# Spreading routing weights over channels by products with a constant 0/1 matrix, in the last stage of a cross-attention and expert kernel

## What is computed

```python
xn = layernorm(x)                                  # x: 8 x 224 x 512
d2 = sum(xn*xn) + sum(p*p) - 2 * xn @ prototypes.T # 32 prototypes
w  = softmax(-sqrt(max(d2, 0)) / t)
topw, topi = top_k(w, 2); topw /= sum(topw)
for slot in range(2):
    h = B[topi[slot]] @ xn                         # rank 16
    y = A[topi[slot]] @ h + bias[topi[slot]]
    out += topw[slot] * y
return x + out
```

## Time and profile before

| what | value |
|---|---|
| median of 3 runs | 996.6 us (992.65 to 997.54) |
| profiled execution: its own time | 998.39 us |
| its span, first to last instruction | 996.7 us |
| mean granted clock of TensorE | 0.967 |
| busy in the span: PE, DVE, ACT, POOL | 90%, 63%, 49%, 25% |
| last stage | from about 798 us to the end |

### The profile page before, as it was taken

One profiled execution on the slowest core, in us unless ns is written; L12 is line 12 of the kernel. 1 busy time (PEld: TensorE's weight loads), 2 busy tenths in 40 slices (PEclk: granted clock), 3 DMA queues, 4 the chain that ended last, 5 costly groups with the idle time before them and its releaser, 6 DMA issues. The chain is left out here.

```text
span 996.7 us, 18525 instructions
## 1 busy us (share of the span) xinstructions
PE 896.3 (90%) x6480; PEld 768.8 (77%) x6480; DVE 628.5 (63%) x1466; ACT 486.6 (49%) x1055; POOL 248.4 (25%) x208
## 2 busy tenths in 40 slices
PE   4899999999999759998899998999999858999996
PEld 4798998989989647777777777777777648788884
DVE  3743643735537068888678887888888645666662
ACT  4211301212212057778677786777787624443431
POOL 0740340621415000033103040033332222223400
PEclk9899999999999969999899998999999978999999
DMA  9646546366444656667756667666778321111201
GB/s 263 213 164 228 193 153 233 135 205 219 173 145 168 167 165 137 145 155 160 155 123 148 149 144 154 147 150 141 184 173 200 91 77 37 57 55 58 70 19 37
DMA packets 96288, 144.36 MB, mean 145 GB/s; under 512 B 7605, under 2 KB 57429, under 8 KB 96226
## 3 DMA queue, kind: packets, MB, share of 16 engines
q1 hardware_dynamic: 93362, 133.56, 49.3%
q0 software_dynamic: 2864, 10.00, 3.7%
HBM read 91.98 MB, written 51.54 MB: 144 GB/s over the span
## 5 line engine op out<-in xcount | busy, mean ns | idle before, releaser
L879 PE MATMUL prob_ps<-ident,scores 112*125 112x112 f32 x1536 | 262.6, 286 | 34.6 <-ACT scores L758 31.9
L879 PEld LDWEIGHTS prob_ps<-ident,scores 112*125 112x125 f32 x1536 | 225.5, 193 | 67.5 <-ACT scores L758 66.8
L805 DVE CUSTOM_DVE_ANT_0 scores<-score_ps,w_in_stage 112x750 f32<-112x750 f32 x256 | 236.3, 923 | 3.2 <-PE score_ps L863 3.2
L758 ACT ACTIVATE scores<-scores,neg_max 112x750 f32<-112x750 f32 x256 | 234.0, 914 | 1.2 <-DVE neg_max L805 1.2
L828 DVE COPY probs_t<-prob_ps 125x336 f32<-125x336 f32 x256 | 128.9, 503 | 85.7 <-PE score_ps L863 73.9
L774 ACT ACTIVATE probs_t<-prob_ps 125x336 f32<-125x336 f32 x256 | 114.7, 448 | 93.2 <-PE prob_ps L879 86.3
L476 DVE TENSOR_TENSOR v_out<-acc,bv_row 125x512 f32<-125x512 f32 x48 | 33.2, 691 | 115.5 <-DMA v_all<-v_out 78.3
L504 PE MATMUL acc<-ctx_hi,w_hi 128*128 128x376 f32 (+1 forms) x256 | 88.9, 347 | 16.9 <-DVE ctx_lo L432 12.9
L419 ACT ACTIVATE q_hi<-q_f 128x448 fp32r<-128x448 f32 x16 | 9.3, 579 | 188.1 <-DVE q_f L483 188.1
L704 POOL COPY rsum_wide<-rsum 112x256 f32<-112x256 f32 x32 | 12.7, 398 | 331.4 <-DVE rsum L835 331.4
L863 PE MATMUL score_ps<-ctx_hi,q_st 96*112 96x376 f32 (+1 forms) x256 | 78.1, 389 | 18.9 <-DVEq L793 12.8
(11 more groups left out here) (153 smaller groups left out, 1667.5 us busy)
## 6 DMA issues: line engine op xcount, KB each, us to landing
ctx_hi<-k_parts SPq DMA_DIRECT2D x48, 375.0 KB, 5.7
ctx_lo<-k_parts SPq DMA_DIRECT2D x48, 375.0 KB, 5.7
ctx_raw<-in_ctx_t SPq DMA_DIRECT2D x32, 375.0 KB, 5.4
k_parts<-k_hi SPq DMA_DIRECT2D x32, 375.0 KB, 3.0
k_parts<-k_lo SPq DMA_DIRECT2D x32, 375.0 KB, 4.0
v_all<-v_out SPq DMA_DIRECT2D x48, 250.0 KB
ctx_raw<-v_all SPq DMA_DIRECT2D x32, 375.0 KB
q_st<-q_parts SPq DMA_DIRECT2D x96, 112.0 KB, 6.6
```

The costliest lines, as they stand in the source:

```text
L758: nc.scalar.activation(scores[:, w % NSC, :], scores[:, w % NSC, :], ACT.Exp, bias=neg_max[:, w % UP:w % UP + 1], scale=-1.0, accum_out=su ...
L805: nc.vector.tensor_tensor_reduce(out=scores[:, w % NSC, :], in0=score_ps[w % 2][:, SCORE_AT:SCORE_AT + S], in1=masked_bias[w // UB % 2][:, ...
L879: last = nc.tensor.transpose(prob_ps[q % NPB][0:SW, s * TW:(s + 1) * TW], scores[:, w % NSC, (BT * j + s) * SW:(BT * j + s + 1) * SW], ide ...
```

## The change

The weight of a channel is the weight of its expert. Before, ScalarE writes `route_wide`, in which each weight stands 16 times, and TensorE transposes it in eight pieces into `big`. Now a constant matrix `spread` (128 rows, 512 columns), built once by POOL at the start of the stage, holds 1 where a row of `route_t` belongs to the column's expert: row n for the rounded weight and row 64 + n for the rest. Four products of `spread` with `route_t` put the weights of all channels into `big`, now two tiles of 128 channels by 224 tokens in each of its two banks, where before it was four tiles of 112 tokens in each. The products stand behind `distances(b+1)` in TensorE's order; the two transposes of `route_st` stay where they were. On ScalarE the copy of `route_ps` to `route_t` moves from behind the squares to ahead of them, and `widen_route` goes. `gate` reads two halves of channels in place of two halves of tokens.

```diff
-        route_wide = sb("route_wide", [TW, TC, NP, RK])
+        spread_f = sb("spread_f", [P, NP, RK])
+        spread = sb("spread", [P, NP, RK], F32R)
...
+            eng.memset(spread_f[:, :, :], 0.0).then_inc(spread_step, 1)
+            for j, first in enumerate((0, 2 * NP)):
+                eng.wait_ge(spread_step, j + 1)
+                eng.affine_select(out=spread_f[:, :, :], in_=spread_f[:, :, :], compare_op=ALU.not_equal, fill=1.0,
+                                  base=-first, pattern=[[-1, NP], [0, RK]], channel_multiplier=1)\
+                   .then_inc(spread_step, 1)
+            eng.wait_ge(spread_step, 3)
+            eng.tensor_scalar(spread[:, :, :], spread_f[:, :, :], 1.0, 0.0, ALU.mult, ALU.add)\
+               .then_inc(spread_ready, 1)
...
-            def widen_route(b):
-                eng.wait_ge(route_ready, b + 1)
-                nc.scalar.activation(route_wide[:, :, :, :],
-                                     route[:, :, :].unsqueeze(3).broadcast_to([TW, TC, NP, RK]),
-                                     ACT.Copy).then_inc(wide_ready, 1)
...
             with eng.Fori(1, LAST) as b:
                 deviation(b + 1)
                 norm(b + 1)
+                copy_route(b)
+                lengths(b + 1)
                 experts(b)
                 route_part(b + 1)
             eng.wait_ge(y_ps_ready, TC * LAST)
+            copy_route(LAST)
             experts(LAST)
...
             def gate(b):
                 eng.wait_ge(h_ready, 2 * b + 2)
                 eng.wait_ge(g_hi_ready, 1 + b)
-                for c in range(TC):
-                    eng.wait_ge(wide_ps_ready, TC * b + c + 1)
-                    last = nc.vector.tensor_tensor(gated[:, :, c * TW:(c + 1) * TW],
-                                                   big[c][:, 0:MT * TW].rearrange("p (m t) -> p m t", m=MT),
-                                                   h_sb[:, :, c * TW:(c + 1) * TW], ALU.mult)
+                for j in range(2):
+                    eng.wait_ge(gate_ps_ready, 2 * b + j + 1)
+                    last = nc.vector.tensor_tensor(gated[:, 2 * j:2 * j + 2, :],
+                                                   big[j][:, 0:2 * T].rearrange("p (m t) -> p m t", m=2),
+                                                   h_sb[:, 2 * j:2 * j + 2, :], ALU.mult)
                 last.then_inc(gated_ready, 1)
...
-            def transpose_routes(b, before):
-                eng.wait_ge(wide_ready, 1 + b + 1)
-                for c in range(TC):
-                    if before is not None:
-                        eng.wait_ge(x1_ready, before + c + 1)
-                    for m in range(MT):
-                        last = nc.tensor.transpose(
...
+            def spread_routes(b, residuals):
+
+                eng.wait_ge(route_t_ready, b + 1)
+                for j in range(2):
+                    if residuals is not None:
+                        eng.wait_ge(x1_ready, residuals + j + 1)
+                    for m in range(2):
+                        tile = 2 * j + m
+                        last = nc.tensor.matmul(big[j][:, m * T:(m + 1) * T],
+                                                spread[:, tile * PM:(tile + 1) * PM, :].rearrange("p n r -> p (n r)"),
+                                                route_t[:, :], start=True, stop=True)
+                    last.then_inc(gate_ps_ready, 1)
...
                 transpose_y(b + 1)
-                transpose_routes(b, 1 + TC * (b + 1))
+                transpose_routes(b)
                 distances(b + 1)
+                spread_routes(b, 1 + TC * (b + 1))
...
             up(LAST - 1, 0)
-            transpose_routes(LAST, None)
+            transpose_routes(LAST)
             up(LAST - 1, 1)
+            spread_routes(LAST, None)
```

More of the change, by code:

```diff
@@ L1030, in finish @@
         route_st_ready = sem("route_st_ready")
-        wide_ready = sem("wide_ready")
+        spread_step = sem("spread_step")
+        spread_ready = sem("spread_ready")
         route_ps_ready = sem("route_ps_ready")
         route_t_ready = sem("route_t_ready")
-        wide_ps_ready = sem("wide_ps_ready")
+        gate_ps_ready = sem("gate_ps_ready")
         h_ps_ready = sem("h_ps_ready")
@@ L1093, in _ @@
         def _(eng):
-            for started in (wide_ready, g_hi_ready, x2_ready):
+            for started in (g_hi_ready, x2_ready):
                 eng.sem_inc(started, 1)
@@ L1114, in norm, with lengths @@
                                          ACT.Copy).then_inc(yt_hi_ready, 1)
+            def lengths(b):
                 for c in range(TC):
@@ L1144, in route_part, with copy_route, experts @@
                 second_weight(b)
-                widen_route(b)
-            def experts(b):
+            def copy_route(b):
                 eng.wait_ge(route_ps_ready, 1 + b + 1)
                 nc.scalar.activation(route_t[:, :], route_ps[:, 0:T], ACT.Copy).then_inc(route_t_ready, 1)
+            def experts(b):
                 eng.wait_ge(gated_ready, b + 1)
@@ L1153, in _ @@
             norm(0)
+            lengths(0)
             distance_root(0)
@@ L1156, in _ @@
             second_weight(0)
-            widen_route(0)
             deviation(1)
@@ L1161, in _ @@
             norm(1)
+            copy_route(0)
+            lengths(1)
             experts(0)
@@ L1271, in routing @@
                 eng.wait_ge(top_step, n + 10)
-                eng.wait_ge(wide_ready, 1 + b)
                 nc.vector.tensor_tensor(route[:, :, :], pick[:, 0, :, :], pick[:, 1, :, :], ALU.add)\
@@ L1400, in transpose_dot, with transpose_routes @@
                 last.then_inc(dot_t_ready, 1)
-            def transpose_routes(b, before):
-                eng.wait_ge(wide_ready, 1 + b + 1)
-                for c in range(TC):
-                    if before is not None:
-                        eng.wait_ge(x1_ready, before + c + 1)
-                    for m in range(MT):
-                        last = nc.tensor.transpose(
[L1409 to L1412, removed]
+            def transpose_routes(b):
                 eng.wait_ge(route_st_ready, 2 * b + 2)
@@ L1457, in _ @@
             eng.wait_ge(small_ready, 1)
+            eng.wait_ge(spread_ready, 1)
             turn_of(0, False)
```

## The result

| what | before | after |
|---|---|---|
| median of 6 runs | 997.07 us (992.65 to 999.41) | 1008.3 us (1006.21 to 1009.96) |
| profiled execution, its time and its span | 998.39, 996.7 us | 1009.32, 1007.6 us |

The ratio is 1.0118, 95% interval 1.0089 to 1.0147: the change makes the kernel slower by about 1.2%. The forecast was 1004.7 us, range 999.5 to 1011.

A forecast was written before the change was run, and what follows sets the result against it. TensorE, 90% busy, was taken to meet a chain from yt_lo to dot almost together. Six turns +6.7, turn 0 +0.9 and tail +0.5 made +8.1 us: 1006.5 profiled, 1004.7 us as median, range 999.5 to 1011.

The forecast's parts named there:

- What bounds the turn: Steady turns: TensorE, busy 20.5 us of each, meets the chain yt_lo to dot at transpose_dot, early by some 0.4 us.
- The price of the gate's wait: Steady turns: gated waits for the spread products behind distances and starts 1.22 us later; six turns +6.7 us.
- The product's price: Spread products on TensorE: like the down products, 0.112 us apart and 0.27 us each, four costing 0.45 us.
- The gain of g_lo: VectorE, steady turns: g_lo starts after POOL's xb ends and takes 1.09 us instead of 1.22 or 1.45.
- Hidden work: Removed transposes (0.77 us a turn), widened copy, moved route_t copy and POOL's set-up (3 to 5 us): all costed at nothing.
- Tail: After the last turn: up(6, 1) ends 1.28 us earlier, but g_hi waits for products and gate; up(7, 0) +0.5 us.
- Turn 0: First turn, clock nearly all at the lower level: the later gate and half-speed products make transpose_dot 0.9 us later.
- A: Rival: larger TensorE holes make the clock fall once a turn, seven turns adding 12 us, about 1017 us; chance 0.06.
- B: Rival: TensorE's work decides, so 0.32 us less a turn and 1.28 in the tail show, 993.1 us; chance 0.04.
- C: Rival: gate late by only half, seven turns giving back 4.3 us, 1000.4 us; chance 0.10.
- D: Rival: POOL's set-up or the first norm adds 1 to 2 us, 1006.5 us; chance 0.05.

The follow-up runs named there:

- the fillers: Changed kernel with eight idle transposes of y2 put back where the transposes of route_wide stood: six turns 134.22 us, ratio 1.0118.
- the early copy alone: Kernel before with only ScalarE's copy of route_t moved ahead of the squares: six turns 127.76 us, ratio 1.0017.
- The two other kernels with a late gate: Kernel before with the wide transposes moved behind distances, ratio 1.0116; changed kernel with eight idle transposes put back, ratio 1.0118.
- the kernel with all mended: Changed kernel with products ahead of distances, last weights in their own tile, dot ahead of g_lo, up(7, 0) waiting only for its own bank: ratio 0.9985.

## Why the prediction was right

**What bounds the turn.** As read: TensorE meets a chain on the other engines, yt_lo to dot, and the chain sets the end. Shown from both sides: eight idle transposes put back into the changed kernel cost nothing, and with dot taken out of the chain TensorE's wait for it is gone and the turns are 5.8 us shorter together. That figure isn't the price of the lateness: the same swap takes 1.8 us off the kernel before, and the 2.6 us that then remain between the two are the products' own time on TensorE. The price of the place is shown most directly by the products moved ahead of `distances` (six turns back to 127.64) and by the wide transposes moved behind it (135.26).

**The price of the gate's wait.** Forecast 1.22 us a turn, measured 1.73 - 0.52 = 1.21. The product's price, taken from the `down` products, held: the four products are issued from 908.87 and gated starts 0.42 us later, as worked out. The gain of g_lo held as well (1.09 us in every turn, and 1.22 and 1.45 before), and so six turns came to +6.5 against +6.7.

**Hidden work.** The removed transposes, the widened copy, the moved copy of route_t and POOL's set-up were costed at nothing; the fillers, the early copy alone and the set-up's rows each show it, and for the widened copy the kernel with the products ahead of `distances`, which has none and is no faster in its turns. The set-up's estimate was 3 to 5 us, it took 3.2.

**Tail.** Forecast +0.5, measured +0.7. The part mis-sized is the first products after a hole: gated starts 0.62 us behind the first product at 991.74, where I took 0.42 from products in a full stream. The wait for route_st and the earlier up(6, 1) came as worked out.

**Turn 0.** Forecast +0.9, and +1.0 between the two first profiles, whose mean granted clock in that turn was 0.83 and 0.84. The traces vary most here, and it goes with the clock: the kernel before took 20.26 us at 0.83 and 18.89 at 0.91. Compared at a like clock, the kernels with a late gate and dot behind it are 1.0 to 1.5 us longer: 21.28, 21.29 and 21.65 at 0.84 against 20.26 at 0.83, and 20.42 at 0.92 against 18.89 and 19.23 (the early copy) at 0.91. The stretch from the stage's start to the end of turn 0 differs by up to 2.5 us between traces of the same program (43.5 and 41.0 for the kernel before), with granted clocks of 0.79 and 0.82 from 812 to 845 us.

**Rivals.** A (clock in the turns): 1.00 in all six, out. B (TensorE's work decides): out for this kernel, by the fillers. Once dot stands ahead of g_lo TensorE does set the turn, but the saving of 0.32 us that B counts on doesn't appear even there: the change then costs 0.44 us a turn. C (partly absorbed): out, gated is late by the whole 1.21 us. D (set-up): out.

**What stays open.** The two measured ratios, 1.0118 and 1.0104, mean 10 to 12 us; turns and tail account for 7.2 and turn 0 for 1.0 to 1.5. The second interval holds the 8.3 us of the stage, the first misses it narrowly. The two other kernels with a late gate show the same: their intervals start at 1.0099 and 1.0097, which is 9.7 us or more, and turns, turn 0 and tail give some 9 for each.

The spans and granted clocks on record for the single executions tell where part of this lies. The span times the mean granted clock is an estimate of what an execution would take at the full clock. Its mean is 974.8 us for the changed kernel's second measurement and 966.3 for the kernel before, timed with it; 974.2 and 974.1 us for the two others, and 966.7 for the kernel before, timed with them. That is 7.4 to 8.5 us more, with a standard error of about 1 us, and near what turns, turn 0 and tail give. The mean times differ by 9.1, 9.5 and 9.7 us. The 0.6 to 2.3 us beyond it are time lost at the lower clock, with a standard error of 1.2 to 1.9 us each. Whether a late gate makes TensorE spend more time at the lower clock, or whether this rest is chance, isn't settled.

## What to carry to other kernels

An operation that only saves work on the busiest engine can still lengthen the turn: before a producer is moved, find what its consumer's engine has queued behind that consumer, and who waits for that. Work taken out ahead of a wait for another engine is worth nothing, and work put into that same hole costs nothing as long as it ends before the wait does, so a new producer belongs there. In the kernel with all mended it ended 0.11 us too late, and once nothing else hid that, it cost 0.13 us a turn. Small operations that the bottleneck waits for should stand in their queue ahead of the long ones, in the gaps of a round trip to another engine; here that shortened six turns by 1.8 us in the trace of the kernel before, which the measured times are too coarse to confirm. And a fix is measured against the old kernel with the same fix: otherwise its own gain is taken for the price of the change.

## Not expected of the hardware

The first products after a hole deliver later than those in a stream: 0.62 us from the first product's start to gated's in the tails of all seven traces that have the products, where TensorE waited 0.45 us before them, and 0.42 in the turns, where it didn't wait; two products lie in between in each case. Half of it shows in their rows: after the hole the first product takes 0.37 us and the second starts 0.21 us behind it, in the stream it is 0.27 and 0.11. What the other half is, the rows don't show.

A shorter hole didn't spare the fall of the clock behind it. In the kernel with all mended, up(7, 0) starts behind a hole of 2.26 us instead of 3.83. By TensorE's timeline:

```profile
986.89 0.46 PE L1369 MATMUL h_ps<-w_hi,g_hi 128*112 128x512 f32 x1 [2.26 <-DVE g_lo L1311]
...
987.41 0.40 PE L1369 MATMUL h_ps<-w_hi,g_lo 128*112 128x512 f32 x1
...
988.41 0.63 PE L1369 MATMUL h_ps<-w_hi,g_lo 128*112 128x512 f32 x1
...
991.29 0.40 PE L1443 MATMUL h_ps<-bst,route_t_last 128*112 128x512 f32 x1
```

The first three products run at 0.46, 0.39 and 0.40 us, then the clock falls with the products running, to 0.63 us each, and is back some 3.3 us later. From up(7, 0) to the end this kernel takes 11.41 us, the kernel before 11.39 with its hole of 3.01 us, the changed kernel 11.33 with one of 3.83. Over all twelve traces that last stretch lies from 11.2 to 12.7 us, and the length of the hole doesn't order them. So the tail's gain over the changed kernel is the 1.5 us up to up(7, 0), and a warmer clock added nothing to it.
